# Three attention layers: VectorE's dependent operations placed one by one between column operations, their completions counted by one pair of semaphores

## What is computed

```python
def _transformer_conv(x, src, tgt, edge_attr, Wq, ...):
    q = (x @ Wq + bq).reshape(N, HEADS, HEAD_DIM)
    k_j = k[src] + e
    alpha = (q[tgt] * k_j).sum(-1) / sqrt(HEAD_DIM)
    m = segment_max(alpha, tgt); a = exp(alpha - m[tgt])
    a = a / segment_sum(a, tgt)[tgt]
    out = segment_sum((v[src] + e) * a[..., None], tgt).mean(axis=1)
    return out + x @ Wskip + bskip
x = _layer_norm(x, ln_in_g, ln_in_b)
for l in range(LAYERS):
    h = elu(_transformer_conv(x, ...))
    x = _layer_norm(x + h, ln_g[l], ln_b[l])
```

## Time and profile before

| what | value |
|---|---|
| median of 3 runs | 7995.07 us (7988.37 to 8000.68) |
| span of the profiled execution | 8002.8 us |
| VectorE busy | 6149.1 us, 77% |
| TensorE busy | 5159.0 us, 64% |
| GpSimd busy | 4947.2 us, 62% |
| ScalarE busy | 4810.4 us, 60% |
| mean granted TensorE clock | 0.822 |

### The profile page before, as it was taken

The page is one execution under the profiler, slowest core; times in us unless marked ns, Lnnn a source line. Parts: engine busy times, 40 slices in busy tenths (PEclk is TensorE's granted clock), DMA queues, the critical chain, the costliest instruction groups (busy, mean ns, idle before and its releaser), DMA issues. The chain is left out here.

```text
span 8002.8 us, 134106 instructions
## 1 busy us (share of the span) xinstructions
PE 5159.0 (64%) x27083; PEld 3725.0 (47%) x27083; DVE 6149.1 (77%) x29318; ACT 4810.4 (60%) x13748; POOL 4947.2 (62%) x4939
## 2 busy tenths in 40 slices
PE   5013333338888768888577777765995777677671
PEld 2012222226666546666355555544554555555551
DVE  9816777748888758888578888885775868888886
ACT  0005888847777747777466666663554656666663
POOL 7776777737777467777375555515764445555553
PEclk8555555559999879999789998987998988888995
DMA  3334655524444334444243333434656843333331
GB/s 97 101 104 98 137 129 127 128 77 151 158 153 161 129 100 157 156 155 155 90 127 131 131 131 131 132 111 138 204 190 220 281 137 109 111 114 104 115 114 33
DMA packets 493460, 1065.71 MB, mean 133 GB/s; under 512 B 230701, under 2 KB 235896, under 8 KB 492658
## 3 DMA queue, kind: packets, MB, share of 16 engines
q1 hardware_dynamic: 341362, 775.06, 29.5%
q0 software_dynamic: 151424, 284.20, 13.4%
HBM read 559.18 MB, written 500.53 MB: 132 GB/s over the span
## 5 line engine op out<-in xcount | busy, mean ns | idle before, releaser
L1656 POOL DMA_INDIRECT xs<-tab,rec x1176 | 1169.1, 994 | 671.1 <-DVE cA L1801 302.9
L1658 POOL DMA_INDIRECT xd<-tab,rec x1176 | 1156.8, 984 | 358.7 <-issue 352.9
L1742 ACT ACTIVATE z<-p_a 128x512 f32<-128x512 f32 x1176 | 697.7, 593 | 558.9 <-PE p_a L1594 551.1
L1736 ACT ACTIVATE st<-xs,cb 128x128 f32<-128x128 f32 x2352 | 804.8, 392 | 201.2 <-DVEq L1850 201.1
L1594 PE MATMUL p_a<-ident,st 128*128 128x128 f32 x2352 | 510.3, 301 | 474.4 <-DVE st L1812 470.2
L1812 DVE SCALAR_TENSOR_TENSOR st<-st,cg 128x128 f32<-128x128 f32 x2352 | 723.5, 348 | 78.6 <-DVE norm L709 52.3
L1687 PE MATMUL p_a<-w_all,xt 128*128 128x256 f32 x2352 | 755.8, 405 | 10.7 <-ACT xt L1727 10.2
L1690 PE MATMUL p_y<-w_all,xt 128*128 128x258 f32 x2352 | 762.2, 407 | 0.6 <-ACT xt L1727 0.5
L2469 POOL DMA_INDIRECT xs<-res,rec x392 | 421.0, 1074 | 508.4 <-PE p_t L2490 319.0
L1801 DVE CUSTOM_DVE_ANT_0 junk<-p_y,xs 128x129 f32<-128x129 f32 x2352 | 582.9, 285 | 115.3 <-PE p_y L1690 113.0
L1594 PEld LDWEIGHTS p_a<-ident,st 128*128 128x128 f32 x2352 | 289.3, 148 | 815.8 <-DVE st L1812 752.9
(11 more groups left out here) (745 smaller groups left out, 16634.0 us busy)
## 6 DMA issues: line engine op xcount, KB each, us to landing
states<-st SPq DMA_DIRECT2D x168, 910.0 KB
own<-tab SPq DMA_DIRECT2D x168, 448.0 KB
tab<-o SPq DMA_DIRECT2D x168, 448.0 KB
runs<-run SPq DMA_DIRECT2D x112, 448.0 KB, 2.8
tab<-out SPq DMA_DIRECT2D x112, 448.0 KB
x<-tab SPq DMA_DIRECT2D x112, 448.0 KB
angles<-st SPq DMA_DIRECT2D x56, 532.0 KB, 2.8
xsrc<-got SPq DMA_DIRECT2D x56, 448.0 KB
```

The lines of the kernel that those rows point to most:

```text
L1656: pool.indirect_dma_start(xs[:, i, j, 0:D], None, table, bass.IndirectOffsetOnAxis(ap=rec[:, i, SRC, j : j + 1], axis=0)).then_inc(got_in[ ...
L1658: pool.indirect_dma_start(xd[:, i, j, :], None, table, bass.IndirectOffsetOnAxis(ap=rec[:, i, PLACE, j : j + 1], axis=0)).then_inc(got_in[ ...
L1736: ins = act.activation(state_of(r, j)[:, h, :], xs[:, c.slot(UB), j, 0:D], ACT.Copy, scale=co.b[:, c.slot(2), h, j : j + 1])
L1742: act.activation(z[:, c.slot(RING), j, :], p_a[two(c, j)][:], ACT.Copy).then_inc(st_copied, 1)
```

## The change

In `conv` alone, VectorE's operations that depend on each other no longer follow one another at once. A new class `Order` counts them all with two semaphores that take turns: `put` marks an operation's increment with its number, `land` waits for that number later, and `begin` clears the semaphore of the turn two back. A new class `PieceNorm` takes the place of `LogNorm`: the aggregates stay where they are written, ScalarE adds epsilon as Ln's bias, so the copy of the means and the radicands are gone, and the root has four operations in place of five, called one by one. Aggregation moves out of the statistics, for the first norm to column six and for the second to column five, in each case behind other work. `Coef.piece` takes the place of `Coef.level` in `conv`, with its signals on the operations themselves and not on separate ones. The shares are now signalled by the last operation of level seven, in column five. The other phases keep `Steps`, `LogNorm` and `Coef.level`.

```diff
+class Order:
...
+    def begin(self, turn):
+        self.now = turn % len(self.sems)
+        if self.count[self.now]:
+            self.eng.wait_ge(self.sems[self.now], self.count[self.now])
+            self.eng.sem_inc(self.passed, 1)
+            self.eng.sem_clear(self.sems[self.now])
+        self.count[self.now] = 0
+    def put(self, ins):
+        ins.then_inc(self.sems[self.now], 1)
+        self.count[self.now] += 1
+        return self.now, self.count[self.now]
+    def land(self, mark):
+        self.eng.wait_ge(self.sems[mark[0]], mark[1])
...
+                pool.memset(k.eps[:], PieceNorm.LN_SCALE * EPS).then_inc(pooled, 1)
...
+class PieceNorm:
...
+    def stats(self, dve, order, v):
+        for r in range(JN):
+            ins = dve.bn_stats(out=self.raw[:, r, :], in_=v[:, r, :])
+        self.taken = order.put(ins)
+    def sums(self, dve, order, c):
+        order.land(self.taken)
+        for r in range(JN):
+            ins = dve.bn_aggr(out=self.mv[:, c.slot(RING), r, :], in_=self.raw[:, r, :])
+        ins.then_inc(self.radicand, 1)
+    def log(self, act, c):
+        i = c.slot(RING)
+        act.wait_ge(self.radicand, c.count(1, 1))
+        act.activation(self.guess[:, i], self.mv[:, i, :, 1], ACT.Ln, bias=self.k.eps[:, 0:1], scale=self.LN_SCALE).then_inc(self.logged, 1)
+        act.wait_ge(self.logged, c.count(1, 1))
+        act.activation(self.guess[:, i], self.guess[:, i], ACT.Exp, scale=-0.5).then_inc(self.guessed, 1)
+    def root(self, n, dve, order, c):
+        i = c.slot(RING)
+        y, t, s = self.guess[:, i], self.newton[:], self.s[:, i]
+        if n == 0:
+            dve.wait_ge(self.guessed, c.count(1, 1))
+            self.at = order.put(dve.scalar_tensor_tensor(t, y, -1.0, y, ALU.mult, ALU.mult))
+            return
+        order.land(self.at)
+        if n == 1:
+            self.at = order.put(dve.scalar_tensor_tensor(t, self.mv[:, i, :, 1], EPS, t, ALU.add, ALU.mult))
+        elif n == 2:
+            self.at = order.put(dve.scalar_tensor_tensor(s[:, 0], t, self.LIFT, y, ALU.add, ALU.mult))
+        elif n == 3:
+            dve.scalar_tensor_tensor(s[:, 1], self.mv[:, i, :, 0], -1.0, s[:, 0], ALU.mult, ALU.mult).then_inc(self.rooted, 1)
...
+    def piece(self, n, dve, order, c, same, scored, exp_in, exped, shares):
+        i, m, z, same = c.slot(2), self.m, self.z, self.wide(same)
+        if n == 0:
+            self.at = order.put(dve.tensor_scalar(self.neg[:, :, 1:], same, -LOW, LOW, ALU.mult, ALU.add))
+            return
+        if n == 4:
+            dve.wait_ge(exped, c.count(1, 1))
+        else:
+            order.land(self.at)
+        if n == 1:
+            dve.wait_ge(scored, c.count(J, J))
+            self.at = order.put(dve.tensor_tensor_scan(self.flat(m[:]), self.flat(self.neg[:]), self.flat(self.A[:, i]), 0.0, ALU.add, ALU.max))
...
+        elif n == 3:
+            dve.tensor_scalar(self.ex[:, 0], self.ex[:, 0], 0.0, None, ALU.min).then_inc(exp_in, 1)
...
+        elif n == 7:
+            dve.tensor_tensor(self.b[:, i], self.a[:, :, 1:], self.rz[:], ALU.mult)
+            ins = dve.tensor_tensor(self.g[:, i], self.h[:], self.rz[:], ALU.mult)
+            if shares is None:
+                self.at = order.put(ins)
+            else:
+                ins.then_inc(shares, 1)
...
-        norm = LogNorm(k, c, 0)
-        norm2 = LogNorm(k, c, 1) if last else None
+        norm = PieceNorm(k, c, 0)
+        norm2 = PieceNorm(k, c, 1) if last else None
...
+                def weight(c):
+                    i = c.slot(UB)
+                    dve.wait_ge(got_in[i], (c.use(UB) + 1) * 32 * J)
+                    wait(dve, weighted, c.count(J, (1 - UB) * J))
+                    at["weight"] = order.put(dve.tensor_copy(xs[:, i, :, 0:1], field(c, WGT).unsqueeze(2)))
...
                 def add_state(c, j):
+                    if j == 0:
+                        order.land(at["beside"])
+                        dve.wait_ge(shares, c.count(1, 1))
...
+                def positive(c):
+                    dve.wait_ge(z_done, c.count(J, J))
+                    at["positive"] = order.put(dve.scalar_tensor_tensor(part(c, 3), part(c, 2), 0.0, part(c, 3), ALU.max, ALU.add))
+                def negative(c):
+                    order.land(at["positive"])
+                    dve.wait_ge(e_out, c.count(1, 1))
+                    dve.scalar_tensor_tensor(part(c, 2), e[:, c.slot(2)], 1.0, part(c, 3), ALU.min, ALU.add).then_inc(resid, 1)
...
+                    order.begin(u)
                     if ahead.there:
-                        i = ahead.slot(UB)
-                        wgt.at(ahead)
-                        dve.wait_ge(got_in[i], (ahead.use(UB) + 1) * 32 * J)
-                        wait(dve, weighted, ahead.count(J, (1 - UB) * J))
-                        wgt(dve.tensor_copy(xs[:, i, :, 0:1], field(ahead, WGT).unsqueeze(2)))
-                        wgt.end()
-                    if mid.there:
-                        coef.at(mid)
-                        dve.wait_ge(scored, mid.count(J, J))
-                    if c.there:
-                        dve.wait_ge(beside_done, c.count(1, 1))
-                        state.at(c)
-                    if c2.there:
-                        res_.at(c2)
-                    def coefficients(n):
-                        if mid.there and n is not None:
-                            co.level(n, coef, dve, mid.slot(2), field(mid, SAME))
+                        weight(ahead)
                     for j in range(J):
-                        if mid.there and j == co.ASK:
-                            coef.land()
-                            dve.nop().then_inc(exp_in, 1)
-                        if mid.there and j == 4:
-                            dve.wait_ge(exped, mid.count(1, 1))
-                        coefficients(co.EARLY.get(j))
-                        if mid.there and j == 6:
-                            dve.nop().then_inc(shares, 1)
+                        if mid.there and j in (0, 1, 4, 5, 6):
+                            level({0: 0, 1: 2, 4: 4, 5: 6, 6: 8}[j], mid)
                         if c.there:
                             add_state(c, j)
+                        if c3.there and j in (1, 2):
+                            norm.root((j - 1) * 3, dve, order, c3)
+                        if last and c5.there and j in (3, 4):
+                            norm2.root((j - 3) * 3, dve, order, c5)
+                        if last and c4.there and j == 5:
+                            norm2.sums(dve, order, c4)
                         if ahead.there:
                             score(ahead, j)
-                        coefficients(co.MIDDLE.get(j))
+                        if c3.there and j == 1:
+                            norm.root(1, dve, order, c3)
+                        if last and c5.there and j == 3:
+                            norm2.root(1, dve, order, c5)
+                        if c2.there and j == 6:
+                            norm.sums(dve, order, c2)
+                        if mid.there and j in (0, 1, 4, 5):
+                            level({0: 1, 1: 3, 4: 5, 5: 7}[j], mid)
                         cz, i = column(k, t, u, 0, j - 2)
                         if cz.there:
-                            if i == 0:
-                                zs.at(cz)
                             add_own(cz, i)
-                            if i == J - 1:
-                                zs.land()
-                                zs.end()
-                        v = part(c2, 2)
-                        if last and c4.there:
...
+                        if c3.there and j == 1:
+                            norm.root(2, dve, order, c3)
+                        if last and c5.there and j == 3:
+                            norm2.root(2, dve, order, c5)
+                        if last and c4.there and j < 3:
+                            affine(j, c4)
+                        if last and c4.there and j == 4:
+                            dve.wait_ge(res_free, c4.count(1, 1))
+                            norm2.stats(dve, order, y2[:, c4.slot(RING)])
                         if j == (0 if last else 3) and c2.there:
-                            dve.wait_ge(e_out, c2.count(1, 1))
-                            res_(dve.scalar_tensor_tensor(v, e[:, c2.slot(2)], 1.0, part(c2, 3), ALU.min, ALU.add))
-                            dve.nop().then_inc(resid, 1)
-                        if j == 1 and c3.there:
-                            root.at(c3)
-                            norm.root(dve, root, c3)
-                            root.end()
+                            negative(c2)
                         if j == 2 and c1.there:
-                            small.at(c1)
-                            small(dve.scalar_tensor_tensor(part(c1, 3), part(c1, 2), 0.0, part(c1, 3), ALU.max, ALU.add))
-                            small.end()
-                        if last and j == 3 and c5.there:
```

(18 more changed lines are left out.)

106 lines of the change are left out of this document (72 added, 34 removed).

## The result

The changed kernel takes **7678.2 us** (median of four runs, 7676.2 to 7684.2) against 7996.0 us (7988.4 to 8000.7) for the kernel before in the same comparison: a ratio of 0.9601, with a 95% interval of 0.9590 to 0.9613. It is faster by 318 us.

A forecast was written before the change was run, and what follows sets the result against it. Layer three was taken as bound by VectorE's own issue chain, layers one and two by GpSimd's gathers. Savings of 4.35 us a chunk (217 us) plus 20 us outside gave 7995.1 - 237 = 7758 us, range 7712 to 7865.

The forecast's parts named there:

- the terms of a turn: VectorE in layer three: four savings sum to 4.35 us a chunk, taking 25.0 to 20.65 us, 217 us in 50 chunks.
- roots, with the gap in front: Two norm roots a chunk of layer three: separated pieces in place of five chained operations gain 2.1 us (1.2 to 2.2).
- statistics: Norm statistics, twice a chunk: the copy of means, the radicands and the wait go, gaining 0.9 us (0.7 to 0.95).
- wide operations: Five 128x896 VectorE operations a chunk: gaps and lost overlap go, gaining 0.9 us (0.5 to 0.95).
- start of a turn: Before a chunk's first level: weights' landing and counter work mostly go, 0.15 us left, gaining 0.45 us (0.2 to 0.6).
- outside these 50 chunks: Layer ends: 12 us in layer three's, 8 in the other two layers', together 20 us (0 to 35).
- layers one and two stay at GpSimd's 18.1 us: Steady turns of layers one and two: GpSimd's 14 gathers a chunk keep them at 18.1 us, so nothing is gained.
- covers: Layer three: GpSimd (18.1 us a chunk), ScalarE (17.0) and TensorE (18.1) stay hidden behind VectorE, costed at nothing.
- ring of engines: Layer three rival: ScalarE or TensorE fall behind in short columns, costing 2 us a chunk; 7857 us, chance 0.08.
- slower case: Rival: the root's first piece waits for ScalarE's guess, holding back score, gathers and products; 8280 us, chance 0.03.
- GpSimd's limit: Rival: layer three is bound by GpSimd, which also waits for records, so nothing moves; 7995 us, chance 0.03.
- count of operations: Rival: landings cost nothing, only six fewer operations matter, 0.98 us a chunk of layer three; 7941 us, chance 0.06.

The follow-up runs named there:

- e2: The changed kernel with the old norm (LogNorm) in its old form and places, all else changed: 7856.1 us.
- e4: The changed kernel with each wide 128x896 VectorE operation waiting for its own landing: 7694.9 us.
- e5: The changed kernel with the old start of a turn (weights land, two increments, two clears): 7697.1 us.
- e6: The changed kernel with layers one and two as before the change, only layer three changed: 7704.3 us.
- e1: The kernel before with only the shorter norm, six operations fewer a turn, each operation still followed by its landing: 7936.4 us, ratio 0.9923.
- e9c: The changed kernel with the root's four operations in a row in layers one and two, layer three as changed: 7652.3 us, ratio 0.9567.
- e10c: The changed kernel with ELU's two wide operations of layers one and two in two parts each: 7657.3 us, ratio 0.9574.

## Why the prediction was right and where it failed

- **What bounds the kernel** was right. Layer three was VectorE's own chain: with fewer landings it gave 281.0 of the 325.5 us, and VectorE is now busy 99% of it.
- **Step that failed: the terms of a turn, 4.35 us.** They came to 5.6 us, 281 us in 50 chunks where 217 were forecast; all were too small, none was wrong in kind. By start-to-start distances of one undisturbed turn of each trace (24.68 and 19.07 us):

| term | forecast | measured | by a run |
|---|---|---|---|
| roots, with the gap in front | 2.1 | 2.4 | without the gap, with statistics 3.16 (e2) |
| statistics | 0.9 | 1.3 | |
| wide operations | 0.9 | 1.1 | 0.71 (e4) |
| start of a turn | 0.45 | 0.57 | 0.59 (e5) |
| rest | 0 | 0.3 | |

- **Roots.** The pieces were put at 0.085 us and cost 0.07 to 0.08. Most of the miss is that not every old step was 0.20 us: the second root held VectorE for 1.43 us, one of its five operations being 0.42 us long.
- **Statistics** were mis-sized most: only the two operations and the wait behind them were counted. Aggregation and statistics also overlap with their new neighbours, 0.49 for 0.58 us and 1.36 for 1.48.
- **Start of a turn.** 0.15 us were kept for the wait, increment and clear that remain. They cost nothing: the weights start 0.07 us behind the copy ahead of them.
- **Step that failed: "outside these 50 chunks" at 20 us, "layers one and two stay at GpSimd's 18.1 us".** It was 44.5 us. Most of the miss is in the ends of layers one and two: from a layer's last gather to the first of the next it took 96.9 and 98.2 us where it had taken 108.9 and 112.2, 26 us less where 8 were forecast. The gathers themselves gave 8.2 us where nothing was (784 of them take 1009.3 and 1008.4 us, before 1011.2 and 1014.7). GpSimd does bound these layers, at 18.0 us a turn, but its gather is no constant: its length depends on what VectorE does meanwhile. Of that no term was made. By e6 some 8 us of these 34 are the spread between executions. The drain gave 7.6 us of its 12.
- **The covers held.** ScalarE and TensorE, costed at nothing, did not take over: VectorE waits 2.3 us for TensorE and 4.8 for ScalarE in 969. GpSimd's, put at 18.1 us a chunk, was thinner than that: its gathers grew with the change, and it needs 18.9. TensorE's granted clock in layer three went up to 0.99 and not down. The ring of engines, the slower case and GpSimd's limit did not come; the count of operations was a part of 60 us (e1).
- **What was to show it.** Turns of 20 to 21.3 us: they are 19.4. A wait for scores of about 100 us: it is 14.3. No gap before the state of column two and pieces under 0.09 us: as forecast.
- **The range** ended at 7712 because its four terms together were allowed no more than 4.70 us a turn, with high ends a tenth above the values taken, and its low ends reached 40% below them; nothing in the rows made the costs on that side so much more certain. The terms measured 5.6 us against that 4.70.

## What to carry to other kernels

Where an engine's gaps bear its own name, price a landing at all that stands around it: the gap, the lost overlap of both neighbours, and the landing and empty signal behind the last step (0.55 us a turn here for two roots); then undo one form at a time, since placing the pieces (0.75 us) was only a third of the root's gain. Apply such an edit only in the stage that the engine bounds: in layers one and two the row was the better order, by 26 us (e9c). And look at whether the bounding engine's own operation has a constant length before it is taken as a floor.

## What was not expected of the hardware

**A gather that begins under a wide VectorE operation waits for it.** GpSimd and VectorE, the changed kernel, layer one, then layer three, then e10c in layer one with the wide operation in two parts:

```profile
1862.16 0.94 POOL L1793 DMA_INDIRECT xd<-tab,rec  x1 [0.30 <-issue]
1863.36 1.08 DVE L1976 SCALAR_TENSOR_TENSOR z<-e,z 128x896 f32<-128x896 f32 x1
1863.41 1.84 POOL L1791 DMA_INDIRECT xs<-tab,rec  x1 [0.31 <-DVE cA L1942]
...
4522.07 0.94 POOL L1793 DMA_INDIRECT xd<-tab,rec  x1 [0.30 <-issue]
4522.11 1.08 DVE L1989 TENSOR_TENSOR y<-y,res 128x896 f32<-128x896 f32 x1
4523.12 1.08 DVE L1971 SCALAR_TENSOR_TENSOR z<-z 128x896 f32<-128x896 f32 x1
4523.32 1.69 POOL L1791 DMA_INDIRECT xs<-tab,rec  x1 [0.30 <-issue]
```

```profile
2061.43 1.15 DVE L1972 SCALAR_TENSOR_TENSOR z<-z 128x512 f32<-128x512 f32 x2
2061.53 1.39 POOL L1793 DMA_INDIRECT xd<-tab,rec  x1 [0.30 <-issue]
```

The gather that began 0.04 us ahead of L1989 took its usual 0.94 us. The one that began 0.20 us into L1971 took 1.69, and the one 0.05 us into L1976 took 1.84 us. Between 1800 and 2340 us of the change 15 of 419 gathers took over 1.2 us, and each of them began inside L1971 or L1976; of the 382 that began under no wide operation none did, 30 under the statistics (L779) among them. Start within the operation plus length is near 1.9 us throughout: 0.3 in gives 1.6, 0.6 gives 1.3, 0.9 gives 1.0. So the gather ends 0.82 us behind the end of that one operation; of its usual 0.94 us only some 0.1 is done before that, and one that begins in the operation's last 0.1 us loses nothing. Parts of 512 and 384 columns cut the longest to 1.39 us (e10c), again 0.8 us behind the first part's end though the second follows without a gap: between two wide operations it does get in.

The Trainium skill has this rule (SBUF — State Buffer, SBUF: two separate sides): a VectorE operation with two inputs in SBUF and a GpSimd operation that reads SBUF share a pair of ports, whoever starts first holds it for the whole instruction, and the other is blocked. For the gather the trace agrees: the wide operations have two such inputs, the statistics have one. The other way round it does not. L1989 began 0.04 us behind a gather and took its 1.08 us, and so did the other wide operations of the three layers that began less than 0.1 us behind one: 125 of them took 1.07 to 1.12 us.

In layers one and two, which GpSimd bounds, this is time: e9c's gathers there are shorter because fewer of them begin early in a wide operation (18 and 18 over 1.2 us in layers one and two, where the change has 29 and 30). Why fewer begin there with the root in a row was not tried by itself. No gather of these layers stands over 0.32 us behind the one before, so they wait for nobody; it is VectorE's wide operations that come at other moments.

**TensorE's clock** in layers one and two went from 0.96 to 0.93 with the change, while in layer three it rose from 0.91 to 0.99, where TensorE is now busy 84% of the time and was 72%. Neither shows in the time: the gathers bound layers one and two and wait for nobody, and VectorE, which bounds layer three, waits only 2.3 us for TensorE.
